# Two more expert tiles ahead of the list, last results stored before the query weights' load, index lists in pieces

## What is computed

```python
x = x + _L0_xattn_ref(_layernorm(x), ctx)      # x + masked (ctx ctx^T) x
x = x + _L0_ffn_ref(_layernorm(x), ...)        # 16-head attention, then 8 experts, top 2 per token
x = x + _L1_xattn_ref(_layernorm(x), ctx, ...) # cross attention, 16 heads of 64
x = x + _L1_ffn_ref(_layernorm(x), ...)        # 16 experts, top 2, and one shared expert

# experts of L0: probs -> top_k 2 -> gate
hid = silu(einsum('td,edf->tef', t, w1)) * einsum('td,edf->tef', t, w3)   # 256 -> 512, "gate" and "up"
y_e = einsum('tef,efd->ted', hid, w2)                                     # 512 -> 256, "down"
y = einsum('ted,te->td', y_e, gate)
```

## Time and profile before

| | us |
|---|---|
| median of three runs | 912.83 |
| the profiled execution | 913.28 |
| its span, first to last instruction | 911.5 |
| TensorE busy | 853.1 |
| VectorE busy | 709.4 |
| ScalarE busy | 604.6 |
| GpSimd busy | 287.2 |

### The profile page before, as it was taken

The page is one execution under the profiler, slowest core; times in us unless marked ns, Lnnn a source line. Parts: engine busy times, 40 slices in busy tenths (PEclk is TensorE's granted clock), DMA queues, the critical chain, the costliest instruction groups (busy, mean ns, idle before and its releaser), DMA issues.

```text
span 911.5 us, 23338 instructions
## 1 busy us (share of the span) xinstructions
PE 853.1 (94%) x7726; PEld 762.7 (84%) x7726; DVE 709.4 (78%) x1990; ACT 604.6 (66%) x1718; POOL 287.2 (32%) x359
## 2 busy tenths in 40 slices
PE   5799989879999999996899999999999999999997
PEld 3677656538999999995898988998889889999996
DVE  4887898776887777786899888777688638888867
ACT  4388899956666676664777667778775327777740
POOL 3865577660000000005554542111023004444420
PEclk9999999979999999997999999999999999999999
DMA  8237700023312311031111121031044933333335
GB/s 316 74 117 269 320 24 26 31 87 112 116 59 70 141 47 59 25 109 50 34 42 36 43 81 67 19 100 36 2 185 191 366 76 92 103 94 100 101 113 200
DMA packets 43319, 94.23 MB, mean 103 GB/s; under 512 B 6112, under 2 KB 29536, under 8 KB 41664
## 3 DMA queue, kind: packets, MB, share of 16 engines
q1 hardware_dynamic: 36336, 73.93, 23.4%
q0 software_dynamic: 6864, 18.80, 6.0%
HBM read 63.53 MB, written 29.17 MB: 102 GB/s over the span
## 4 chain that ended last, share of the span: by engine, by line
PE 65%; DVE 8%; issue 2%; ACT 2%; DMA 1%; POOL 0%; ACTq 0%; SPq 0%; DVEq 0%; POOLq 0%
PE ps L1023 17%; PE ps L829 11%; PE ps L830 10%; PE ps L831 10%; PE ps L1116 3%; PE ps L1140 3%; PE ps L1126 3%; PE ps L1198 2%; DVE BIGR L2084 1%; PE ps L1224 1%; PE ps L995 1%; PE ps L996 1%; DMA ys_dram<-BIG 1%; DVE X L2119 1%; ACT BIGR L1395 1%
## 5 line engine op out<-in xcount | busy, mean ns | idle before, releaser
L829 PE MATMUL ps<-BIGR 128*128 128x256 f32 (+1 forms) x946 | 292.0, 309 | 7.5 <-DVE BIGR L2084 3.1
L831 PE MATMUL ps<-BIGR 128*128 128x256 f32 (+1 forms) x898 | 255.8, 285 | 0.0
L830 PE MATMUL ps<-BIGR 128*128 128x256 f32 (+1 forms) x722 | 211.7, 293 | 0.0
L829 PEld LDWEIGHTS ps<-BIGR 128*128 128x128 f32 x946 | 180.7, 191 | 14.3 <-issue 9.8
L1023 PE MATMUL ps<-BIG 128*128 128x128 f32 x1424 | 177.3, 275 | 0.0
L831 PEld LDWEIGHTS ps<-BIGR 128*128 128x128 f32 x898 | 171.1, 191 | 0.7
L1023 PEld LDWEIGHTS ps<-BIG 128*128 128x128 f32 x1424 | 168.1, 192 | 0.1
L830 PEld LDWEIGHTS ps<-BIGR 128*128 128x128 f32 x722 | 138.5, 192 | 1.8
L2328 POOL DMA_INDIRECT BIG<-ys_dram,YI x32 | 35.3, 1102 | 218.2 <-DMA ys_dram<-BIG 210.5
L1565 ACT ACTIVATE BIG<-ps,BIG 128x128 f32<-128x128 f32 x256 | 91.0, 383 | 13.2 <-DVE BIG L2164 12.9
L2313 POOL DMA_INDIRECT xs_dram<-TT,PI x64 | 65.5, 1023 | 86.2 <-ACT PI L1375 72.3
(11 more groups left out here) (304 smaller groups left out, 1873.4 us busy)
## 6 DMA issues: line engine op xcount, KB each, us to landing
BIG<-in_wgu SPq DMA_DIRECT2D x2, 6144.0 KB, 19.1
BIG<-in_wd SPq DMA_DIRECT2D x2, 4096.0 KB, 22.5
BIG<-xs_dram SPq DMA_DIRECT2D x47, 129.5 KB, 2.1
BIG<-xs_dram SPq DMA_DIRECT2D x37, 128.0 KB, 2.0
ys_dram<-BIG SPq DMA_DIRECT2D x37, 128.0 KB, 2.0
BIG<-in_wkv SPq DMA_DIRECT2D x2, 2048.0 KB, 9.5
kv_dram<-BIG SPq DMA_DIRECT2D x16, 256.0 KB, 2.1
BIG<-in_wgu SPq DMA_DIRECT2D x2, 2048.0 KB, 9.8
```

The costliest lines, as they stand in the source:

```text
L829: pe.matmul(o, l[0], r[0], start=start, stop=False)
L830: pe.matmul(o, l[0], r[1], start=False, stop=False)
L831: return pe.matmul(o, l[1], r[0], start=False, stop=stop)
```

## The change

AHEAD goes to 4 and COUNTED to 9, so NT0 to 35 and PAIRED to 14. The early tiles 0 and 3 take their banks from the ring `misc`, 1 and 2 from `s`; tile 0's row transposes follow `qkT` of the last block instead of `s`. Gate, up and down products are cut into four phases each, of one product of 256 columns. `a_route` is cut into four phases and `places` into eight, each of the eight behind the weights of one of the single tiles 16 to 23. The row transposes of the ordinary tiles from j = 2 on and the first gate product are ordered behind the last early up product, the gate product of j = 2 behind the last early down product. `load_q` follows the last tile's store (`ys`) instead of its down product. `a_xs` waits for block 11's context product instead of block 9's, since four context rows are overwritten. The lead table has new values throughout; its early tiles' entries are 0, and their due times are 500, 700, 900 and 900 (600 for `a_route`) instead of 400.

```diff
-AHEAD = 2
-COUNTED = 10
-AHEAD_DUE = 400
+AHEAD = 4
+COUNTED = 9
+AHEAD_DUE = (500, 700, 900, 900)
+A_DUE = 600
...
-    p.add("DVE", 4400, ("places",), ("wv", 0, 8), due=4000)
+    for i, ns in enumerate((800, 950, 950, 950, 1250, 950, 950, 1250)):
+        p.add("DVE", ns, ("places", i), ("wv", 0, PAIRED + 2 + i), due=-2000)
...
 def ahead_phases(p):
-    p.add("DVE", 2200, ("a_route",), ("rb", 0, COUNTED - 1), due=AHEAD_DUE)
+    for i in range(4):
+        p.add("DVE", 650, ("a_route", i), ("rb", 0, COUNTED - 1), due=A_DUE)
     for i in range(AHEAD):
         def add(engine, ns, name, *after, banks=(), **kw):
-            p.add(engine, ns, (name, i), *after, banks=[("s", (q, i)) for q in banks], due=AHEAD_DUE + 20 * i, **kw)
-        add("SP", 700, "a_xs", ("a_route",), ("sc", 0, COUNTED - 1), ("ctx", COUNTED - 1), ("load_w0b",), late=2200)
-        add("PE", 600, "a_reg", ("a_route",), ("load_w0b",))
-        add("PE", 220, "a_xT", ("a_xs", i), ("s", NB - 1), banks=["a_xT_e"])
-        add("ACT", 310, "a_xT_e", ("a_xT", i), ("a_up1", i - 2))
-        add("PE", 860, "a_gate0", ("a_xT_e", i), ("a_reg", i), banks=["a_silu"])
-        add("PE", 860, "a_gate1", ("a_gate0", i))
-        add("PE", 860, "a_up0", ("a_gate1", i), banks=["a_hm"])
-        add("PE", 860, "a_up1", ("a_up0", i))
+            p.add(engine, ns, (name, i), *after, banks=[("s" if i in (1, 2) else "misc", (q, i)) for q in banks], due=AHEAD_DUE[i] + 20 * i, **kw)
+        add("SP", 700, "a_xs", ("a_route", 3), ("sc", 0, COUNTED - 1), ("ctx", COUNTED + 2), ("load_w0b",), late=2200)
+        add("PE", 600, "a_reg", ("a_route", 3), ("load_w0b",))
+        add("PE", 220, "a_xT", ("a_xs", i), ("s" if i else "qkT", NB - 1), banks=["a_xT_e"])
+        add("ACT", 310, "a_xT_e", ("a_xT", i), ("a_up3", i - 2))
+        for which, bank in (("gate", "a_silu"), ("up", "a_hm")):
+            for x in range(4):
+                before = (f"a_{which}{x - 1}", i) if x else ("a_gate3", i) if which == "up" else ("a_xT_e", i)
+                add("PE", 430, f"a_{which}{x}", before, ("a_reg", i), banks=[] if x else [bank])
...
-        add("PE", 860, "a_down0", ("a_hT_e", i), banks=["a_y"])
-        add("PE", 860, "a_down1", ("a_down0", i))
-        add("ACT", 330, "a_y", ("a_down1", i))
+        for x in range(4):
+            add("PE", 430, f"a_down{x}", (f"a_down{x - 1}", i) if x else ("a_hT_e", i), banks=[] if x else ["a_y"])
+        add("ACT", 330, "a_y", ("a_down3", i))
...
-            add("PE", 220, "xT", ("xs", r, j), banks=[("xT", "xTl")])
+            p.add("PE", 220, ("xT", r, j), ("xs", r, j), *[("a_up3", AHEAD - 1) for _ in range(j > 1)],
+                  banks=[("xT0", ("xTl", r, j))], due=3 * j)
...
-            p.add("PE", 1440, ("gate", r, j), ("xTl", r, j0), ("wv", r, j), ("xTl", r, j0 + 1), banks=[("gate0", ("silu", r, j))], due=3 * j)
+            p.add("PE", 1440, ("gate", r, j), ("xTl", r, j0), ("wv", r, j), ("xTl", r, j0 + 1),
+                  *[("a_up3", AHEAD - 1) for _ in range(j == 0)], *[("a_down3", AHEAD - 1) for _ in range(j == 2)], banks=[("gate0", ("silu", r, j))], due=3 * j)
...
-    p.add("SP", 100, ("load_q",), ("down", 0, NT0 - 1), late=8000)
+    p.add("SP", 100, ("load_q",), ("ys", 0, NT0 - 1), late=8000)
...
-                at = k * 2 * F0 + (F0 if which == "up" else 0)
-                m = pe.matmul(ps(*key)[:, :], AXT[i % 2][:, k * 128:k * 128 + 128],
-                              WGU[:, bass.ds(expert[i] * (4 * F0) + at, F0)], start=k == 0, stop=k == 1)
-                if k == 1:
+                at = k * 2 * F0 + (F0 if which == "up" else 0) + half * D
+                m = pe.matmul(ps(*key)[:, half * D:half * D + D], AXT[i % 2][:, k * 128:k * 128 + 128],
+                              WGU[:, bass.ds(expert[i] * (4 * F0) + at, D)], start=k == 0, stop=k == 1)
+                if x == 3:
                     m.then_inc(*fills(*key))
...
-                    sp.wait_ge(*full("ctx", COUNTED - 1))
+                    sp.wait_ge(*full("ctx", COUNTED + 2))
```

More of the change, by code:

```diff
@@ L372, in cross_phases @@
 def cross_phases(p):
-    p.add("SP", 100, ("load_kv",), ("down", 0, PAIRED - 1), ("a_down1", AHEAD - 1), due=0, late=12000)
-    p.add("SP", 100, ("load_q",), ("down", 0, NT0 - 1), late=8000)
+    p.add("SP", 100, ("load_kv",), ("down", 0, PAIRED - 1), ("a_down3", AHEAD - 1), due=0, late=12000)
+    p.add("SP", 100, ("load_q",), ("ys", 0, NT0 - 1), late=8000)
     p.add("ACT", 100, ("tanh",), ("load_kv",), ("hh", 0, NT0 - 1))
@@ L412, in cross_phases @@
         for b in (2 * j, 2 * j + 1):
-            add("POOL", 2550, ("ga", 0, b), ("ys", 0, NT0 - 1), ("a_ys", AHEAD - 1), ("places",), ("pro1", b - 2),
+            add("POOL", 2550, ("ga", 0, b), ("ys", 0, NT0 - 1), ("a_ys", AHEAD - 1), ("places", 7), ("pro1", b - 2),
                 late=4000 if b < 2 else 2800)
@@ L1879, in a_route, with add_up @@
                 tiles = OHW[0].rearrange("p a n -> p (a n)")[:, 0:E * AHEAD].rearrange("p (n j) -> p n j", n=E)
-                v.tensor_tensor(nn, CNT[:, COUNTED, 0:E], ecap[0], ALU.subtract).then_inc(dv, next_step("dve"))
-                then()
-                v.tensor_tensor(tiles, nn.rearrange("p (n o) -> p n o", o=1).broadcast_to([128, E, AHEAD]),
-                                cst["cmp"][:, 1:1 + AHEAD].rearrange("p (o j) -> p o j", o=1).broadcast_to([128, E, AHEAD]),
-                                ALU.is_ge).then_inc(dv, next_step("dve"))
-                then()
-                v.tensor_reduce(steps[0][:, 8:16], tiles, AX, ALU.add).then_inc(dv, next_step("dve"))
-                for i in range(3):
-                    then()
+                inc, before = [steps[3][:, 8 - x:16 - x] for x in range(2)]
+                def add_up(i):
                     v.tensor_tensor(steps[i + 1][:, 8:16], steps[i][:, 8:16], steps[i][:, 8 - 2 ** i:16 - 2 ** i],
@@ L1891, in a_route @@
                 then()
-                v.tensor_scalar(steps[3][:, 8:16], steps[3][:, 8:16], float(AHEAD), None, ALU.min).then_inc(dv, next_step("dve"))
-                then()
-                inc, before = [steps[3][:, 8 - x:16 - x] for x in range(2)]
-                v.scalar_tensor_tensor(out=ahead_row, in0=before, scalar=-128.0, in1=ecap[0], op0=ALU.mult,
-                                       op1=ALU.add).then_inc(dv, next_step("dve"))
-                v.tensor_scalar(w1, inc, cst["j"], None, ALU.is_le).then_inc(dv, next_step("dve"))
@@ L1898, in a_route @@
-                then()
-                v.tensor_reduce(te, w1, AX, ALU.add).then_inc(dv, next_step("dve"))
-                v.scalar_tensor_tensor(out=behind, in0=inc, scalar=128.0, in1=ahead_row, op0=ALU.mult,
-                                       op1=ALU.add).then_inc(dv, next_step("dve"))
-                then()
-                v.scalar_tensor_tensor(out=w1, in0=iota[0][:, 0:E], scalar=te, in1=ahead_row, op0=ALU.is_equal,
-                                       op1=ALU.mult).then_inc(dv, next_step("dve"))
@@ L1946, in places @@
-                then()
-                v.tensor_tensor(RP[:, 32:64], RP[:, 32:64], RP[:, 64:96], ALU.mult).then_inc(dv, next_step("dve"))
-                then()
-                v.tensor_tensor(Y1[:, :], Y1[:, :], RP[:, 32:64], ALU.add).then_inc(dv, next_step("dve"))
-                then()
-                for i, t in enumerate((ahead_row, behind)):
-                    v.tensor_tensor(OHw, oh, t.rearrange("p (o n) -> p o n", o=1).broadcast_to([128, 2 * NB, E]),
-                                    ALU.mult).then_inc(dv, next_step("dve"))
+                if step_ == 0:
+                    v.tensor_scalar(C, RP[:, 96 + 7:96 + 16], float(PAIRED // 2), None, ALU.min).then_inc(dv, next_step("dve"))
+                    v.scalar_tensor_tensor(out=singles_at, in0=RP[:, 112 + 7:112 + 15], scalar=-128.0, in1=behind, op0=ALU.mult,
+                                           op1=ALU.add).then_inc(dv, next_step("dve"))
@@ L1954, in places @@
                     then()
-                    v.tensor_reduce(RP[:, 32 * i:32 * i + 32], OHw, AX, ALU.add).then_inc(dv, next_step("dve"))
+                    v.scalar_tensor_tensor(out=pairs_at, in0=C[:, 0:E], scalar=-256.0, in1=behind, op0=ALU.mult,
+                                           op1=ALU.add).then_inc(dv, next_step("dve"))
+                    v.scalar_tensor_tensor(out=singles_at, in0=C[:, 1:E + 1], scalar=256.0, in1=singles_at, op0=ALU.mult,
+                                           op1=ALU.add).then_inc(dv, next_step("dve"))
```

141 lines of the change are left out of this document (83 added, 58 removed), and 27 rows, old and new, of the table LEAD.

## The result

The changed kernel takes **933.65 us** (median; 931.95 to 934.03) against 913.56 of the kernel before in the same set: a ratio of 1.0223, 95% interval 1.0204 to 1.0242. I had forecast 897.0 in 888 to 909. So the sign was wrong, and 36.65 us lie between forecast and measurement.

The account below looks back on a forecast made before the run. TensorE, busy 94% of the span, was taken as the bound, so only less work or filled idle time pays. Terms -9.4 - 1.4 - 5.0 = -15.8 from 912.83 gave 897.0 us, range 888 to 909.

Parts of the forecast that it names:

- The new lead table: Orders everywhere change; little to win after the step to the cross attention: 0 us, ends -3 and +3.
- new TensorE gaps after 430: Sign of a wrong forecast: TensorE idling anew after 430 us would mean the lead values cost more than allowed.
- A pair fewer: First experts: two ordinary tiles fewer remove one pair, 9.40 us with TensorE as the limit: -9.4 us.
- the early tiles: End of first attention: two more early tiles fit TensorE's idle time, first ordinary gate product 1.4 us earlier; ends -2.7, +0.2.
- no room: Rival: ScalarE feeds early tiles only after block 15, so they come no earlier; -5.1 us, 908; chance 0.15.
- The low level through the early tiles: Rival: TensorE stays at 1.2 GHz from 187 on, all four early tiles run there; +7.3 us, 920; chance 0.07.
- my slower rival: Four early tiles all run with TensorE at 1.2 GHz after first attention; +7.3 us, 920; chance 0.07.
- The load behind the stores: Step to cross attention: query weights' load after last result stores lets store and gather land earlier; -5.0 us (4.7 to 6.0).
- my lower bound: Step to cross attention: gather lands only with the query weights' end at 413.3 instead of 418.06, gaining 4.7 us.
- Function tables: ScalarE at the early tiles: two more table loads, 1.40 us each, covered by other early products; 0, ends 0 and +2.8.
- The pieces: Early products cut to 256 columns: +0.8 us at the most, taken as 0.
- the rings of banks: Early tiles use two bank rings, so tile 0 needn't wait for block 15's score banks: 0 us.

Follow-up runs that it names:

- the first run: Changed kernel with one lead value, of the second experts' result copies (y), set from -106 to 0, giving DVE's old order there: 907.93 us, ratio 0.9931 to before.

## Why the prediction was wrong, step by step

*The new lead table: the step that failed.* I priced it at 0, ends -3 and +3, because behind the second dip the slices left little to win and the order could not be read from the table. That looked at what there was to gain, not at what there was to lose: a stretch in which TensorE is busy for 9 tenths or more stands still if an order on another engine closes a loop longer than its work. Measured: +25.7 (933.65 - 907.93), at one place, from one value. This term alone outweighs all that the others could win. I had named "new TensorE gaps after 430" as what would show this term wrong, and they did, but I gave it no chance and no upper bound from a mechanism, so neither the range nor the 0.07 for slower held it. The bound could have been worked out from DVE's timeline of before: from y by the two index steps to hl are 0.33 + 0.24 + 0.07 us, and with 0.59 on to the down product and 0.98 from there to y (the changed kernel's) that is 2.21; the copy and its read, put into this loop, lift it over 2.72 even with before's shortest wait (0.34 + 0.20 more).

*A pair fewer: -9.4, and the early tiles: -1.4 on top.* The pair's 9.4 is not contradicted, but four early tiles instead of two came out at 907.93 against 907.5, so the two terms together are about 0, where I had -10.8. The mis-sized term is the room for early work: I counted 4.4 us of idle time in a window from 173, of which 3 would stay, but no early product starts before 189.08. That is the rival "no room", to which I gave 0.15, with its mechanism: ScalarE feeds the early tiles only once block 15 is through. The run that moves this copy forward starts the early products 3.0 us earlier, counted from block 14, and the ordinary ones 1.4.

*The low level through the early tiles* came for some 3 us only: the granted clock in the changed kernel's trace is 0.50 from 191 to 193, after TensorE had been idle for 1.57 us ahead of 189.08, 1.00 from 194 on and 0.90 over 189 to 206, against 0.50 in 189 to 202 before, and no eight products of an early tile take 6.5 us as in the earlier trace rows. The kernel became slower for another reason than my slower rival.

*The load behind the stores: -5.0 (4.7 to 6.0).* Right: 6.2 by the medians of the run that undoes it, 4.9 in its trace (26.94 - 22.00). The store lands in 1.71 us as written, and the gather's second transfer takes 4.96 instead of 2.68: it lands at 413.75, right behind the weights' load, which was my lower bound. The changed kernel's transfers by queue (packets, MB, share), from 407 to 411.4 us and from 412 to 414.2; q1 is the weights' queue, q0 the gather's:

```profile
q1 hardware_dynamic: 229, 1.74, 95.8%
```

```profile
q0 software_dynamic: 181, 0.48, 60.8%
q1 hardware_dynamic: 19, 0.03, 3.9%
```

The gather's first transfer was issued at 407.51, and none of the 192 packets of its first four transfers ran up to 411.4; in the run that has the load first, they run from 1.7 us after the issue on. The Trainium skill (DMA: Bandwidth & Descriptors, Queues, rings and completion order) has the engines take turns between queues; this trace does not bear that out, since the gather sat out nearly all of the weights' load. `places` would have eaten the gain if left where it was: shown, at 411.85.

*Function tables: 0, ends 0 and +2.8.* The two more loads came, at 195.44 and 198.20, 1.28 us each. The run without them took only 0.6 us from TensorE's wait there, so 0 was near. The silu behind the second one starts at 199.49, right at the load's end, so the drain of 1.38 us that the Trainium skill adds (ScalarE: Activation LUTs, What ACT_TABLE_LOAD costs) does not show here either.

*The pieces, the rings of banks* show no cost of their own in the early rows: 3.62 us for an early tile's sixteen pieces at 196.59, against 3.60 for the eight wide products in the earlier trace rows, and 1.89 for eight down matmuls as there.

The sum by what the runs show: about 0 for the pair and the early tiles and -6.2 for the load, against -5.4 in the first run, where all but the order in the second experts is the changed kernel's; with +25.7 for that order, -6.2 gives +19.5, and the kernel is 20.1 slower. The two traces say where the 5.4 us arise. Block 14's transposition on DVE stands at 182.40 in before and at 182.34 in after. The last down product of the first experts in before, and the first query product in after:

```profile
401.13 0.36 PE L829 MATMUL ps<-BIGR 128*128 128x256 f32 x1
```

```profile
424.00 0.35 PE L834 MATMUL ps<-BIGR 128*128 128x256 f32 x1 [1.81 <-DVE BIGR L2099]
```

Up to the last down product (401.79 in after) the changed kernel is 0.7 us later, so the pair and the early tiles have won nothing there. From it to the first query product (427.70 in the earlier trace rows) it wins 4.4, and from there to the landmark (712.26 and 706.85) 1.7 more, in the cross attention; none of my terms priced these, and no run here explains them.

## What to carry to other kernels

A stretch where the main engine is saturated is not safe ground: before pricing a new order at nothing, follow the loop on each helping engine from the main engine's product back to the next one, and compare its sum with the product's pace; here 2.21 became 3.25 against 2.72. A step with idle time of its own in front of it (here a register read) belongs where the engine waits anyway, or its read belongs ahead. And work pulled forward fills a gap only if its first feeder, here a copy on a full engine, can run before the gap. And before starts in two traces are compared, compare a mark ahead of the change: here the same step lies up to 4 us apart.

## What the hardware showed that I had not expected

DVE's read of a number from SBUF into a register costs idle time according to what runs ahead of it: 0.59 us behind a step of 0.16 us, 0.20 to 0.33 behind one of 0.42, and some 0.14 behind one of 0.69 (the next step starts at 803.06, 0.06 behind its end; without the read, in the changed kernel, it starts at 802.07, 0.08 ahead of that end). From the start of the step ahead to the start of the step behind the read it is 0.75 us, 0.62 to 0.75 and 0.75. It looks as if the read starts with the step ahead of it and needs some 0.7 us; that was only read off the timelines, not tried by itself.

After the gap of 3.27 us ahead of the last down product of the first experts, TensorE's granted clock stood at 0.50, the 1.2 GHz level, from 402.3 to 405.5, so this gap cost more than its length: by an estimate from these rows, 3.2 busy us at the low level are 1.6 at the full one.

A gather can stand behind a load on another queue: in the changed kernel it was issued at 407.51, and its packets ran only behind 411.4, when 1.9 of the load's 2.1 MB were through.
